# Block order of a mixture-of-experts phase, and the output stage drawn into it

## The reference, cut to what matters

```
T = B * L                                   # 32 * 1024 tokens
C = max(1, math.ceil(CAPACITY_FACTOR * T / E))
idx = jnp.argmax(probs, axis=-1)            # one expert of 8 for each token
pos = (jnp.cumsum(one_hot, axis=0) * one_hot).sum(-1) - 1
kept = pos < C                              # an expert takes at most C = 5120 tokens
buf = zeros(E, C, D).at[idx, pos_safe].set(x, mode='drop')
hmid = relu(einsum('ecd,edf->ecf', buf, w1) + b1)      # 128 -> 512
ybuf = einsum('ecf,efd->ecd', hmid, w2) + b2           # 512 -> 128
y_tok = ybuf[idx, pos_g] * (prb * kept)
t = t + nan_to_num(y_tok)
return _from_tokens(t, x)                   # tokens back to channels x positions
```

## Time and profile before

| | |
|---|---|
| median of 3 runs | 2505.41 us (2498.07 to 2508.59) |
| the profiled execution | 2497.93 us, of which 2496.2 us are the span of the core |
| share of the span busy | PE 88%, DVE 75%, ACT 47%, POOL 40% |
| first products of the expert phase | 1846.57 us after the span's start |
| last product of the expert phase | about 2375 us |
| first load of the output stage | 2391.54 us |
| mean granted TensorE clock | 0.934 of full speed (2.4 GHz) |

### The profile page before, as it was taken

The page is one execution under the profiler, slowest core; times in us unless marked ns, Lnnn a source line. Parts: engine busy times, 40 slices in busy tenths (PEclk is TensorE's granted clock), DMA queues, the critical chain, the costliest instruction groups (busy, mean ns, idle before and its releaser), DMA issues. The chain is left out here.

```text
span 2496.2 us, 42793 instructions
## 1 busy us (share of the span) xinstructions
PE 2197.8 (88%) x14047; PEld 1785.5 (72%) x14047; DVE 1878.5 (75%) x6062; ACT 1167.5 (47%) x2184; POOL 1009.8 (40%) x1262
## 2 busy tenths in 40 slices
PE   2699999999999999999999999998749999999945
PEld 1477777777777777777777777777648888888834
DVE  3468878887878888778888788887548888887822
ACT  0144544544434444445444445444237776766712
POOL 2012443334443334533334433343436565555510
PEclk9699999999999999999999999999869999999965
DMA  6711211112211112211112111111046666666568
GB/s 228 275 35 43 67 46 44 52 47 54 64 44 52 44 47 59 58 43 52 44 52 68 45 46 49 44 48 49 18 123 184 192 187 190 180 189 175 139 223 315
DMA packets 163512, 243.97 MB, mean 98 GB/s; under 512 B 31039, under 2 KB 110478, under 8 KB 163296
## 3 DMA queue, kind: packets, MB, share of 16 engines
q1 hardware_dynamic: 141408, 192.68, 27.0%
q0 software_dynamic: 17280, 31.84, 3.9%
q10 hardware_dynamic: 4608, 16.78, 1.7%
HBM read 115.95 MB, written 95.56 MB: 85 GB/s over the span
## 5 line engine op out<-in xcount | busy, mean ns | idle before, releaser
L995 PE MATMUL pvp<-va,pT 128*128 128x129 f32 x4096 | 536.2, 287 | 1.4 <-ACT pT L556 1.4
L995 PEld LDWEIGHTS pvp<-va,pT 128*128 128x128 f32 x4096 | 514.9, 203 | 11.3 <-ACT pT L556 3.0
L1124 POOL DMA_INDIRECT token_rows<-res x284 | 312.9, 1102 | 234.8 <-DVE res L1235 162.3
L654 DVE TENSOR_REDUCE mxs<-mxp 128x1 f32<-128x512 f32 x512 | 333.9, 683 | 21.7 <-PE mxp L873 17.5
L1281 PEld LDWEIGHTS e_yp<-w2s,hid 128*128 128x128 f32 x2272 | 294.6, 192 | 71.0 <-ACT hid L1170 48.7
L1281 PE MATMUL e_yp<-w2s,hid 128*128 128x128 f32 x2272 | 306.2, 278 | 27.8 <-ACT hid L1170 26.8
L470 POOL DMA_INDIRECT expert_slots<-rows,slot_i x256 | 273.8, 1069 | 97.5 <-issue 91.7
L427 POOL TENSOR_TENSOR rstd<-var,neghalf 128x4 f32<-128x4 f32 x128 | 131.0, 1023 | 396.5 <-DVE negm L645 396.1
L556 ACT ACTIVATE pT<-stp 128x512 f32<-128x512 f32 x512 | 277.6, 595 | 17.2 <-issue 9.4
L967 PE MATMUL stp<-qhl,klh 128*128 128x512 f32 x512 | 237.0, 463 | 27.4 <-ACT pT L556 14.2
L1170 ACT ACTIVATE hid<-e_hp,b1c 128x512 f32<-128x512 f32 x284 | 193.1, 680 | 144.6 <-PE e_hp L1273 132.6
(11 more groups left out here) (222 smaller groups left out, 4278.3 us busy)
## 6 DMA issues: line engine op xcount, KB each, us to landing
w1p<-w_parts SPq DMA_DIRECT2D x71, 512.0 KB
expert_slots<-fill SPq DMA_DIRECT2D x32, 660.0 KB, 12.7
e_rows<-expert_slots SPq DMA_DIRECT2D x71, 264.0 KB
w2s<-in_w SPq DMA_DIRECT2D x71, 256.0 KB
xs<-in_x SPq DMA_DIRECT2D x32, 512.0 KB, 3.7
token_rows<-rows SPq DMA_DIRECT2D x32, 512.0 KB
f_rows<-token_rows SPq DMA_DIRECT2D x32, 512.0 KB, 5.8
out<-f_cols ACTq DMA_DIRECT2D x32, 512.0 KB, 5.4
```

The costliest lines, as they stand in the source:

```text
L654: v.reduce_max(mxs[:, qt, n % 2:n % 2 + 1], mxp[n % 2][:], AX).then_inc(s["mx_read"], 1)
L995: last = mm(pvp[qt % 2][:, 0:VA], pT[c][:, kt, n * P:(n + 1) * P], va[k][:, kt, :], start=(kt == 0), stop=(kt == NT - 1))
L1124: g.indirect_dma_start(out=tokens, out_offset=bass.IndirectOffsetOnAxis(ap=res[n % 2][:, q, TOKEN:TOKEN + 1].bitcast(I32), axis=0), in_=re ...
```

## The change

1. **Order of blocks.** The table puts the blocks in the order of groups of four batches (SPAN): first all blocks that the tokens of batches 0 to 3 reach into, of all eight experts, then those that batches 4 to 7 add, and so on. So the rows of group g are final when the first 8(g + 1) + 7 blocks are stored. The counts at the end of each group are kept as `snap` during the token phase, and the table takes 19 instructions on all 128 partitions instead of 14 on one.
2. **Output inside.** `output_program` is gone. From block FIRST = 20 on each block n does half a batch of the output, x = n - 20: TensorE turns it (`turn_out`, four transposes into the bank `tp[1]`) between `layer1(n, 3)` and `layer2(n, 2)`; ScalarE copies the even halves, VectorE the odd ones (`evict`); SP loads the rows (`load_done`) and stores the result (`store_out`), both on its own queue, in every second block. The halves 51 to 63 come after the last block, with six banks in turn.
3. **Buffers.** Four buffers of `e_rows` instead of two, loaded three blocks ahead instead of one; the rows of a block are turned in the single bank `tp[0]`, so `turn(n)` waits until `turned(n - 1)` has copied it.

```diff
 NBLKS = T // BLK + E - 1
 WBUF = 4
+RBUF = 4
+OBUF = 4
+SPAN = 4
+SPB = SPAN * N // BLK
+NSEG = B // SPAN * E
+FIRST = 20
 FILL_ROWS = 10
 NFILL = E * CAP // (P * FILL_ROWS)
 NO_TOKEN = 1 << 24
...
             chain(g.affine_select(out=upto[:], in_=upto[:], pattern=[[1, E], [-1, E]], compare_op=ALU.is_ge, fill=0.0,
                                   base=0, channel_multiplier=0))
-            chain(g.iota(level_i[:], pattern=[[0, E], [BLK, NBLK]], base=0, channel_multiplier=0))
+            chain(g.iota(level_i[:], pattern=[[BLK, NBLK]], base=0, channel_multiplier=0))
             chain(g.tensor_copy(level[:], level_i[:]))
-            chain(g.iota(kidx_i[:], pattern=[[1, NBLKS], [0, E]], base=0, channel_multiplier=0))
-            chain(g.tensor_copy(kidx[:], kidx_i[:]))
+            chain(g.iota(seg_i[:], pattern=[[0, B // SPAN], [1, E]], base=0, channel_multiplier=0))
+            chain(g.tensor_copy(seg_expert[:, 0:NSEG], seg_i[:]))
+            chain(g.memset(seg_expert[:, NSEG:NSEG + 1], 0.0))
+            chain(g.iota(blk_i[:], pattern=[[0, 1]], base=0, channel_multiplier=1))
+            chain(g.tensor_copy(blk[:, 0:1], blk_i[:]))
+            chain(g.tensor_scalar(blk[:, 1:2], blk[:, 0:1], float(BLK), 0.0, ALU.mult, ALU.add))
+            chain(g.tensor_scalar(shift_row[:, NSEG:NSEG + 1], blk[:, 1:2], -1.0, float(E * CAP), ALU.mult, ALU.add))
+            chain(g.memset(reach[:, 0:1], 1.0))
+            chain(g.memset(reach[:, NSEG + 1:NSEG + 2], 0.0))
             chain(g.memset(qkscale[0:U, :], 0.125))
             chain(g.memset(qkscale[U:P, :], 1.0))
             chain(g.memset(img[:], 0.0))
...
+                ng = B // SPAN
+                flat = "p g e -> p (g e)"
+                dve.wait_ge(s["slot_ready"], B)
+                step(v.tensor_scalar(held[:], snap[:].rearrange(flat), float(CAP), None, ALU.min))
+                step(v.tensor_tensor(past[:], held[:].unsqueeze(2).to_broadcast([P, NSEG, NBLK]),
+                                     level[:].unsqueeze(1).to_broadcast([P, NSEG, NBLK]), ALU.is_gt))
+                step(v.reduce_sum(filled[:].rearrange(flat), past[:], AX))
+                step(v.tensor_copy(fresh[:, 0, :], filled[:, 0, :]))
+                step(v.tensor_tensor(fresh[:, 1:ng, :], filled[:, 1:ng, :], filled[:, 0:ng - 1, :], ALU.subtract))
+                step(v.tensor_tensor(tri[:], upto[:].unsqueeze(1).to_broadcast([P, ng, E, E]),
+                                     fresh[:].unsqueeze(2).to_broadcast([P, ng, E, E]), ALU.mult))
+                step(v.reduce_sum(ends[:].rearrange(flat), tri[:].rearrange("p g e f -> p (g e) f"), AX))
+                step(v.reduce_sum(total[:], filled[:], AX))
+                step(v.tensor_tensor(ends[:, 1:ng, :], ends[:, 1:ng, :],
+                                     total[:, 0:ng - 1].unsqueeze(2).to_broadcast([P, ng - 1, E]), ALU.add))
+                step(v.tensor_scalar(reach[:, 1:NSEG + 1], ends[:].rearrange(flat), blk[:, 0:1], None, ALU.is_le))
+                step(v.tensor_tensor(inside[:], reach[:, 0:NSEG + 1], reach[:, 1:NSEG + 2], ALU.subtract))
+                step(v.tensor_tensor(held[:], filled[:].rearrange(flat), ends[:].rearrange(flat), ALU.subtract))
+                step(v.scalar_tensor_tensor(out=shift_row[:, 0:NSEG], in0=seg_expert[:, 0:NSEG], scalar=float(NBLK), in1=held[:],
+                                            op0=ALU.mult, op1=ALU.add))
+                step(v.tensor_scalar(shift_row[:, 0:NSEG], shift_row[:, 0:NSEG], float(BLK), None, ALU.mult))
+                step(v.tensor_tensor(picked[:, 0, :], inside[:], shift_row[:], ALU.mult))
+                step(v.tensor_tensor(picked[:, 1, :], inside[:], seg_expert[:], ALU.mult))
+                step(v.reduce_sum(blk[:, 2:4], picked[:], AX))
+                step(v.tensor_tensor(block_row[:], blk[:, 2:3], blk[:, 1:2], ALU.add))
+                step(v.tensor_copy(block_expert[:], blk[:, 3:4]))
...
+                    if b % SPAN == SPAN - 1:
+                        v.tensor_copy(snap[:, b // SPAN, :], run[:, 0, :])
                     v.tensor_tensor(slot_i[k][:], r8[:, 4, :], r8[:, 5, :], ALU.add).then_inc(s["slot_ready"], 1)
...
+        stored, out_stored = ([sem(f"{n}{k}") for k in range(2)] for n in ("e_stored", "f_stored"))
+        rows_loaded = [sem(f"e_rows_loaded{k}") for k in range(RBUF)]
         w_loaded = [sem(f"e_w_loaded{k}") for k in range(WBUF)]
+        f_loaded = [sem(f"f_loaded{k}") for k in range(OBUF)]
 
         def wait_rows(eng, n):
 
-            eng.wait_ge(rows_loaded[n % 2], n // 2 * 16 + 16)
+            eng.wait_ge(rows_loaded[n % RBUF], n // RBUF * 16 + 16)
 
         def wait_weights(eng, n):
 
             eng.wait_ge(w_loaded[n % WBUF], n // WBUF * 64 + 64)
+
+        def wait_results(eng, n):
+
+            for k in range(2):
+                eng.wait_ge(stored[k], (n + 1 - k) // 2 * (G * 16))
 
         block = ctx.enter_context(nc.Block())
 
         @block.sync
         def _(sp):
             def load_rows(n):
-                row = sp.value_load(block_row[0:1, n:n + 1], min_val=0, max_val=E * CAP)
-                sp.dma_start(rows[n % 2][:].rearrange("p g d -> p (g d)"),
-                             slots[bass.ds(row, BLK)].rearrange("(p g) d -> p (g d)", p=P)).then_inc(rows_loaded[n % 2], 16)
+                row = sp.value_load(block_row[n:n + 1, 0:1], min_val=0, max_val=E * CAP)
+                sp.dma_start(rows[n % RBUF][:].rearrange("p g d -> p (g d)"),
+                             slots[bass.ds(row, BLK)].rearrange("(p g) d -> p (g d)", p=P)).then_inc(rows_loaded[n % RBUF], 16)
 
             def load_weights(n):
-                e = sp.value_load(block_expert[0:1, n:n + 1], min_val=0, max_val=E - 1)
+                e = sp.value_load(block_expert[n:n + 1, 0:1], min_val=0, max_val=E - 1)
                 k = n % WBUF
                 for dst, src in ((w1p[k][:].bitcast(F32), w1parts[bass.ds(e, 1)].rearrange("o p a f -> (o p) a f")),
                                  (w2s[k][:], w2[bass.ds(e, 1)].rearrange("o (c p) d -> p (o c) d", p=P)),
@@ -1093,21 +1135,50 @@
                                  (b2r[k][:], b2[bass.ds(e, 1)].rearrange("o d -> (o d)").partition_broadcast(P))):
                     sp.dma_start(dst, src).then_inc(w_loaded[k], 16)
 
+            def load_done(b):
+
+                if b < 0 or b >= B:
+                    return
+                wait_results(sp, min(b // SPAN * SPB + SPB + E - 1, NBLKS))
+                if b >= OBUF:
+                    sp.wait_ge(s["f_turned"], (b - OBUF) * 2 + 2)
+                sp.dma_start(done_rows[b % OBUF][:], tokens[bass.ds(b * N, N)].rearrange("(p t) c -> p t c", p=P))\
+                    .then_inc(f_loaded[b % OBUF], 16)
+
+            def store_out(b):
+
+                if b < 0 or b >= B:
+                    return
+                sp.wait_ge(s["f_lo_ready"], b + 1)
+                sp.wait_ge(s["f_hi_ready"], b + 1)
+                sp.dma_start(out[b:b + 1].rearrange("o c n -> (o c) n"), cols[b % 2][:]).then_inc(out_stored[b % 2], 16)
+
             load_rows(0)
             load_weights(0)
-            load_rows(1)
+            for n in range(1, RBUF):
+                load_rows(n)
             load_weights(1)
             for n in range(NBLKS):
-                if n >= 1 and n + 1 < NBLKS:
+                if n >= 1 and n + RBUF - 1 < NBLKS:
 
                     sp.wait_ge(s["e_kept"], n)
-                    load_rows(n + 1)
+                    load_rows(n + RBUF - 1)
                 if n + 2 < NBLKS:
                     if n >= 2:
 
                         sp.wait_ge(s["e_y_done"], n - 1)
                         sp.wait_ge(s["e_yb_ready"], (n - 1) * 2)
                     load_weights(n + 2)
+                if n >= FIRST - 2 and (n - FIRST) % 2 == 0:
+                    load_done((n - FIRST) // 2 + 1)
+                    store_out((n - FIRST) // 2 - 2)
+            step = (NBLKS - 1 - FIRST) // 2
+            for b in range(step - 1, B):
+                load_done(b + 3)
+                store_out(b)
+            for k in range(2):
+                sp.wait_ge(stored[k], (NBLKS + 1 - k) // 2 * (G * 16))
+                sp.wait_ge(out_stored[k], B // 2 * 16)
 
         @block.gpsimd
         def _(pool):
@@ -1125,6 +1196,23 @@
                         ap=res[n % 2][:, q, TOKEN:TOKEN + 1].bitcast(I32), axis=0), in_=res[n % 2][:, q, 0:C], in_offset=None,
...
+        def bank(x):
+
+            if x < NBLKS - FIRST:
+                return tp[1]
+            return (tp[1], tp[0], hp[0], hp[1], hp[2], hp[3])[(x - (NBLKS - FIRST)) % 6]
+
+        def evict(x, copy, eng):
+
+            if x < 0 or x >= 2 * B:
+                return
+            b, e = x // 2, x % 2
+            eng.wait_ge(s["f_turned"], x + 1)
+            if b >= 2:
+                eng.wait_ge(out_stored[b % 2], b // 2 * 16)
+            copy(cols[b % 2][:].rearrange("c (m e) -> c e m", e=2)[:, e, :], bank(x)[:])\
```

(64 more changed lines are left out.)

113 lines of the change are left out of this document (8 added, 105 removed).

## The result

The changed kernel takes 2429.0 us, median of 4 runs (2422.77 to 2432.19), against 2505.41: a ratio of 0.9696 [0.9667, 0.9725], 76 us faster. The profiled execution, the quickest of the four, has a span of 2421.0 us. The forecast was 2434 for the median and 2428.7 for the span.

What follows compares the result with a forecast made beforehand. TensorE bounds the token and expert phases, stores the output stage. 2496.2 - 84 + 10 + 3 + 5 - 2 + 0.5 = 2428.7 us of span, 2434 us as median; likeliest range 2418 to 2450, whole range 2392 to 2480.

Steps and rivals of the forecast that it cites:

- The bound and the tail: Output stage after the last product (T): hangs on last scatter's landing and seven stores, ends T + 37, gain 84 us.
- the lower bound of T + 31: Output stage: earliest program end, 31 us after the end of the last product (T), from 11.3 + 20.
- What the phase takes on: Expert phase: transposes +10, copies +3, DMA +5, row buffers -2 us; with constants +0.5, the sum's additions.
- my upper end of 18 us: Expert phase, TensorE: four more transposes in 51 blocks at 0.35 us cost 18 us if all shows; 10 taken.
- the 8 us of cover: Expert phase: TensorE's idle time at the late ReLU hides part of the transposes, so 10 of 18 us count.
- Four row buffers: -2 us: Expert phase: four buffers of `e_rows` end ScalarE's 7.8 us of waits for rows, of which TensorE saw little: -2 us.
- DMA: 5 us, 0.8 to 0.9: Expert phase: output loads and stores delay scatters and loads, 5 us; DMA share 0.8 to 0.9 from block 20.
- Rival 1: Expert phase: the late ReLU goes away, blocks 6.80 us, then 0.35 more; -28 in place of +10, 2396 us; chance 0.22.
- Rival 2: Expert phase: copies and DMA show; 18 transposes, 15 copies, 20 late stores and contention; 2469 us; chance 0.19.
- my 13 and 5: Expert phase: 10 us for transposes plus 3 for copies, and 5 us for DMA transfers.
- Rival 3: Expert phase: stores queue behind weights, ScalarE waits over 2.8 us in each of 25 block pairs; 2505 us and more; chance 0.03.
- Rival 4: Expert phase: `load_done` waits for late scatters, output rows come late and hold TensorE; 25 us lost, 2459 us; chance 0.05.

Runs made afterwards that it cites:

- second group: Later runs on one chip, both kernels unchanged plus two variants: kernel before 2491.7 us, changed kernel 2413.1 us, ratio 0.9687.
- first group: Earlier runs on one chip, four variants of the changed kernel against the kernel before (2415.2 us): 2381.4, 2403.5, 2382.4 and 2357.6 us.

## Why the prediction was right

**The bound and the tail: right.** The end hangs on the landing of the last scatter and seven stores, as forecast. The term was -84 us and measured -89.7; the lower bound of T + 31 was nearly reached (31.4 instead of 37). SP's turn came at T + 12.5, not 14, and the seven stores took (2421.0 - 2402.6) / 7 = 2.6 us each, not 3.06. That a scatter takes 3 us to land no row of before shows; in the chains above it is 2.1 and 2.5 us, which changes nothing.

**What the phase takes on: right in sum, 13.8 us against 16.5** (16.5 in the second group, too), **but not in its parts.** That the errors of the parts cancel so well is luck, and so in part is the match itself, given the single long blocks. The runs without a late ReLU give the parts bare:

| | from | us |
|---|---|---|
| transposes and copies | 509.4 - 486.6 | 22.8 |
| loads and stores | 518.4 - 509.4 | 9.0 |
| order, buffers, one bank | blocks of 6.78 us without a gap | 0 |

22.8 us in 51 blocks are 0.45 each; one more turn without a copy costs (7.67 - 7.22) = 0.45 again (two chips, neither with a late ReLU). So the copies are hidden and the transposes are the whole price, 0.45 us and not 0.35: my upper end of 18 us was too low. The timeline of TensorE without transfers shows what I had misread:

```profile
2103.04 1.05 PE L1381 MATMUL e_yp<-w2s,hid 128*128 128x128 f32 x8
2103.93 0.60 PE L1357 MATMUL e_tp<-e_ident,e_u 128*128 128x128 f32 x4
2104.29 0.48 PE L1371 MATMUL e_hp<-e_up,w1p 128*128 128x512 f32 x1
2106.65 0.60 PE L1399 MATMUL e_tp<-e_ident,f_rows 128*128 128x128 f32 x4
2107.09 1.06 PE L1381 MATMUL e_yp<-w2s,hid 128*128 128x128 f32 x8
```

The four transposes of `turn_out` begin 0.44 us before the next product. Those of `turn` begin 0.36 us before theirs, the 0.35 of the earlier trace rows, but the eight products ahead of them take 0.89 us from start to start, where eight ahead of a `layer1` take 0.81 (2105.06 to 2105.87): the other 0.08 us fall before the start that I read from.

The transfers cost 9.0 us because their stores miss the moment of need by tenths of a microsecond, and not by their volume alone. With each half turned twice (on the first group's chip) the blocks are longer, the copy needs its buffer 12.1 us after SP's turn began (median), the same transfers make ScalarE wait for 1.3 us only, and the phase is 532.6 - 509.4 = 23.2 us longer than without transfers and with one turn: the second turn (51 x 0.45) and nothing more. That is why it is only 14.2 us longer than the changed kernel's.

So with the late ReLU, too, where blocks are longer, most of these 9 us do not show (0.9 and 5.8 us of waits for stores). That, and idle time of TensorE that the transposes fill, are the two reasons that the traces show for the same additions costing 14 to 17 us there and not 31.8. TensorE's wait for the late ReLU fell by 8.7 us in the first pair of profiles and by 6.7 in the second, beside the 8 us of cover that the prediction took. In the first pair the parts nearly add up (22.8 + 0.9 - 8.7 = 15.0 against 13.8), in the second they don't (22.8 + 5.8 - 6.7 = 21.9 against 16.5); single blocks of 9 to 13 us in both traces may hold the rest, which isn't shown.

**Four row buffers: -2 us was wrong as a price.** They looked like a small gain because I asked what two buffers cost today. With the output inside, two cost 8.5 against 7.4 us a block from the twentieth on (two chips, neither with a late ReLU); the phases are 572.7 and 518.4 us, 54 apart. With two, the kernel is 0.5% faster than before, and not 2.5% or 3%: four buffers are what makes the change pay.

**DMA: 5 us, 0.8 to 0.9.** The share measured 0.77, a little less, and the price was nothing to speak of in the first profile (0.9 us of waits), 9.0 us where the blocks are shorter.

**Rival 1** did not happen through the change: the ReLU is late in the changed kernel, too. On two occasions it was late in no kernel that was traced. The kernel before wasn't traced there, but its time fits: the start of the changed kernel (1796.5), a phase of 486.6 and a tail of 121.1 make 2404 us of span by estimate, and 2407.7 were measured. There the blocks took 6.80 and 7.40 us, not 7.15, and the gain was smaller, 59 us against 79: 15 of these 20 us are the higher price of the output inside (31.8 against 16.5), part of it cover that is missing and part stores that come late. **Rival 2** had part of the truth there: 22.8 us for transposes and copies (it said 33) and 9.0 for the transfers (it said 20), against my 13 and 5. **Rival 3** named the right wait, ScalarE's for the store of two batches before, and its time of need of 12 us was right in the first profile; without the late ReLU it is 11.2, and the store misses it by 0.7 us on average in 13 turns, not by the 2.8 in all 25 that it takes to lose everything. **Rival 4** did not occur: TensorE waited for `f_rows` only after the last block.

**Still open:** why the ReLU starts 1.2 us after its products have ended. On one chip it was there in every trace of one group of runs and in none of the next, and together with it a token phase that is 44 us longer; the first trace after puts 31.7 us of ScalarE's waits in front of the ReLU, in 13 times, down to a release from an unknown place ("remote").

## What to carry to other kernels

A stage that hangs on stores can be drawn into a stage that hangs on TensorE at the price of its TensorE work, if transfers are ordered early enough (here 22.8 us of 31.8; the rest was stores that landed tenths of a microsecond late): count how many buffers ahead the old streams need once the new one stands in the same queue. Before that, it pays to order the work so that the late stage can start on finished results without a barrier: order, buffers and the missing barrier together were 24 of 59 us. What remains is a chain of latencies (last result, scatter, load, turn, store), which shrinks by making the last group small and by putting nothing that is ready behind a wait. The price of an inserted piece of work is the lengthening of the whole stretch around it, and not the distance from its own start to the next one. Idle time of the bounding engine that a forecast uses as cover must be one that the code makes; here it was one that came and went.

## What was not expected of the hardware

- One and the same kernel took 2491.9 and 2407.7 us on the same chip in two groups of runs, 3.4% apart, with the mean granted clock in the expert phase of the changed kernel, traced both times, at 1.00. Its phase was 543.1 and 518.4 us; what its two traces show different there is the ReLUs that start late (blocks of 7.21 and 6.80 us before the twentieth) and single long blocks, the longest of 11.8 and 13.1 us, in the slower one.
- Four 128 x 128 transposes between two products cost 0.45 us of a full TensorE. Where 0.35 lie between their first start and the next product's, the products ahead of them take the rest, 0.08 us longer than ahead of another product.
- Stores that landed 11.2 us after SP's turn began (median; 10.7 to 13.0) cost 9.0 us in 51 blocks where the copy needed them after 11.2. With each half turned twice (another chip), in blocks 0.44 us longer, where the need came after 12.1, ScalarE waited 1.3 us in all.
